# Making the mixture panels on GpSimd alone, with one round of it moved ahead of another panel's low halves

## What is computed

```
xn = layernorm(x)
h = xn @ W.T + b                              # graph part: degree-normalised sum of h over the edges
gnn = segment_sum(norm * h[col], row)
q, k, v = xn @ Wq.T + bq, xn @ Wk.T + bk, xn @ Wv.T + bv
mix = (relu(q P) (relu(k P)^T v)) @ Wo.T + bo   # linear attention, 16 heads of 64
x = x + gnn + mix
x = x + ffn(layernorm(x))                      # 8 experts, gate and up, silu, down, routing weights
```

## Time and profile before

| | |
|---|---|
| median of 3 runs | 1085.24 us (1084.15 to 1086.44) |
| the profiled execution | 1084.87 us, of it the span 1083.1 us |
| TensorE busy | 1062.4 us, 98% |
| VectorE busy | 536.7 us, 50% |
| ScalarE busy | 290.0 us, 27% |
| GpSimd busy | 349.5 us, 32% |
| mean granted clock of TensorE | 0.995 |

### The profile page before, as it was taken

One profiled execution on the slowest core, in us unless ns is written; L12 is line 12 of the kernel. 1 busy time (PEld: TensorE's weight loads), 2 busy tenths in 40 slices (PEclk: granted clock), 3 DMA queues, 4 the chain that ended last, 5 costly groups with the idle time before them and its releaser, 6 DMA issues.

```text
span 1083.1 us, 15216 instructions
## 1 busy us (share of the span) xinstructions
PE 1062.4 (98%) x5527; PEld 882.0 (81%) x5527; DVE 536.7 (50%) x1152; ACT 290.0 (27%) x445; POOL 349.5 (32%) x225
## 2 busy tenths in 40 slices
PE   8999999999999999999959999999999999999998
PEld 7887778887878888888848888887788888888887
DVE  6944666676641222332427657967334212214684
ACT  5320211112232234321222223267222212202221
POOL 4000011122130025375500249955108744500151
PEclk9999999999999999999989999999999999999999
DMA  7303011222233386645595567766045556205912
GB/s 270 98 30 108 13 35 53 62 69 72 70 121 88 141 313 244 234 146 174 169 324 207 204 189 215 197 170 183 1 161 196 206 179 218 64 24 224 378 66 110
DMA packets 135933, 163.17 MB, mean 151 GB/s; under 512 B 8534, under 2 KB 102578, under 8 KB 130738
## 3 DMA queue, kind: packets, MB, share of 16 engines
q1 hardware_dynamic: 135282, 160.33, 44.9%
q10 hardware_dynamic: 576, 1.84, 0.4%
HBM read 107.70 MB, written 54.45 MB: 150 GB/s over the span
## 4 chain that ended last, share of the span: by engine, by line
PE 94%; DVE 3%; DMA 1%; SPq 1%; ACT 1%; issue 1%; ACTq 0%
PE ps L1890 9%; PE ps L1892 9%; PE ps L1891 9%; PE ps L2225 7%; PE ps L2226 7%; PE ps L2227 7%; PE ps L2136 6%; PE ps L2137 6%; PE ps L2138 6%; PE ps L2159 4%; PE ps L2165 4%; PE ps L2056 3%; PE ps L2058 3%; PE ps L2057 3%; PE ps L1900 2%; PE ps L2002 2%
## 5 line engine op out<-in xcount | busy, mean ns | idle before, releaser
L1890 PE MATMUL ps<-w_hi,xnH 128*128 128x512 f32 x464 | 184.6, 398 | 0.0
L1892 PE MATMUL ps<-w_hi,xnL 128*128 128x512 f32 x464 | 180.9, 390 | 0.0
L1891 PE MATMUL ps<-w_lo,xnH 128*128 128x512 f32 x464 | 180.7, 389 | 0.0
L892 POOL TENSOR_TENSOR acc<-acc,cw 128x320 f32<-128x320 f32 x40 | 35.7, 893 | 252.6 <-ACT cw L1096 251.4
L1890 PEld LDWEIGHTS ps<-w_hi,xnH 128*128 128x128 f32 x464 | 87.1, 188 | 18.7
L1892 PEld LDWEIGHTS ps<-w_hi,xnL 128*128 128x128 f32 x464 | 87.1, 188 | 18.6
L1891 PEld LDWEIGHTS ps<-w_lo,xnH 128*128 128x128 f32 x464 | 87.2, 188 | 17.1
L1841 DVE TENSOR_TENSOR prd<-ps,wB 128x512 f32<-128x512 f32 (+1 forms) x24 | 14.2, 593 | 144.5 <-PE ps L2227 105.4
L2056 PE MATMUL ps<-xnH,w_hi 128*128 128x512 f32 (+1 forms) x192 | 68.1, 355 | 0.0
L2225 PE MATMUL ps<-x2H,guH 128*128 128x512 f32 (+1 forms) x192 | 67.7, 352 | 0.4 <-ACT wT L1334 0.4
L2226 PE MATMUL ps<-x2L,guH 128*128 128x512 f32 (+1 forms) x192 | 67.6, 352 | 0.0
(11 more groups left out here) (474 smaller groups left out, 2243.8 us busy)
## 6 DMA issues: line engine op xcount, KB each, us to landing
cR<-c_d SPq DMA_DIRECT2D x20, 640.0 KB, 5.0
foldin<-in SPq DMA_DIRECT2D x32, 256.0 KB, 2.7
guR<-in SPq DMA_DIRECT2D x16, 512.0 KB, 6.8
w_raw<-in SPq DMA_DIRECT2D x14, 512.0 KB, 6.3
c_d<-cw SPq DMA_DIRECT2D x40, 160.0 KB
wdq<-in SPq DMA_DIRECT2D x6, 1024.0 KB, 7.6
qR<-qT_d SPq DMA_DIRECT2D x20, 256.0 KB, 4.9
wd_d<-wd1H SPq DMA_DIRECT2D x5, 1024.0 KB, 6.5
```

The lines of the kernel that those rows point to most:

```text
L1890: pe.matmul(target, xnH[:, kc, cols], wH[w][:, kc, :], start=(kc == 0), stop=False)
L1891: pe.matmul(target, xnH[:, kc, cols], wL[w][:, kc, :], start=False, stop=False)
L1892: mm = pe.matmul(target, xnL[:, kc, cols], wH[w][:, kc, :], start=False, stop=(kc == KC - 1))
```

## The change

- ACT no longer makes the high parts of the mixed panels: `mix_high` and `MIX_AT` are gone. POOL makes them itself with a `tensor_copy` in front of the low part of the same step, and with the two waits that ACT's had (low part of the step before made, high part of the step before stored).
- On POOL, `panel_lo(1)` moves from ahead of the four rounds to between the first and the second round.
- In SyncE's queue, `load_panel(1, wh_pan[1])` and the wait for the last q stores move behind the first four block loads and the first four `own` loads. The wait for M's stores stays ahead of them.

```diff
@@ SyncE
             sp.wait_ge(*made(("q", 23)))
-            load_panel(1, wh_pan[1])
             for p in range(2):
                 sp.wait_ge(m_st[p], 48 * KC)
-            for c in range(3):
-                sp.wait_ge(q_st[c], 16 * KC)
...
             for t in range(4):
                 load_own(t)
+            load_panel(1, wh_pan[1])
+            for c in range(3):
+                sp.wait_ge(q_st[c], 16 * KC)
             for n in range(16):
@@ GpSimd
-            panel_lo(1)
-
             for k in range(4):
...
                     pool.wait_ge(wd_mix, 4 * k + 4)
+                    if n:
+                        pool.wait_ge(wd_lo, n)
+                        pool.wait_ge(wd_st[0], 16 * n)
+                    pool.tensor_copy(mixH[:], mixR[room_of][:]).then_inc(wd_hi, 1)
                     pool.wait_ge(wd_hi, n + 1)
...
+                if k == 0:
+                    panel_lo(1)
@@ ScalarE
-            def mix_high(n):
-                act.wait_ge(wd_mix, 4 * (n // 4) + (1, 3, 3, 4)[n % 4])
-                if n:
-                    act.wait_ge(wd_lo, n)
-                    act.wait_ge(wd_st[0], 16 * n)
-                act.activation(mixH[:], mixR[MIX_MADE[n % 4][0]][:], ACT.Copy).then_inc(wd_hi, 1)
...
-            MIX_AT = {3: (0, 1), 4: (2, 3), 6: (4,), 7: (5, 6), 8: (7,), 9: (8,), 10: (9, 10), 11: (11,), 12: (12,),
-                      13: (13, 14), 14: (15,)}
...
                     h_high(hf, t)
-                    for n in MIX_AT.get(NT * hf + t, ()):
-                        mix_high(n)
```

## The result

| | before | changed |
|---|---|---|
| median of 20 runs | 1085.2 us | 1086.42 us |
| lowest to highest | 1084.15 to 1086.44 | 1084.87 to 1088.05 |
| ratio, 95% interval | | 1.0013 (1.0007 to 1.0018) |
| profiled execution, span | 1083.1 us | 1083.1 us |

The medians are 1.2 us apart and the ratio is 1.0013: within 0.2%, but on the slow side. The forecast was 1086.1 us.

A forecast was written before the change was run, and what follows sets the result against it. The bound was the end of the 16 steps (537.56), then 21.7 us to the first of the seven products. Terms -2.8 + 1.0 + 0 + 1.9, plus 0.8 for overlaps, gave +0.9 us: 1086.1 us, range 1081.3 to 1091.5.

The forecast's parts named there:

- round 2: From round 1's last combination to round 2's: 13.8 us to the last low store against 13.83 before, so 0.
- overlaps, put apart: Added 0.8 us for loads stretched beside DVE's work and more POOL operations on the chain in each round.
- The bound: End of the 16 steps sets the time, us for us, through TensorE's 11.1 us wait; at most about 10 us winnable.
- The rival by which the q loads are bound by tile 9's h: A tie for another reason: no move of the chain of steps would show in the time; no chance given.
- The copy: POOL's cast of 128 by 512, 16 times on the chain, put at 0.63 us each.
- The dearer copy: Rival: POOL's copy at 0.95 us adds 5.1 us, giving 1091.2; copy or overlaps dearer had chance 0.22.
- the rival that would have made the time 1088.3: POOL's copy takes the skill's 769 ns, making the sum 2.2 us longer; chance 0.10.
- Round 0 and the low halves: POOL starts at 449.2, 11.7 us earlier; panel 1's 10.83 us of low halves leave 2.8 us at round 1's checkpoint.
- The rival of a kept lead: Panel 1's low halves do not hold round 1's start, -8.8 us remains, time 1076; chance 0.03 with other surprises.
- The links: Copy to copy on POOL: copy 0.63, hop 0.1, store 2.65, so 3.4 us; 3.2 in round 3.
- the rival of faster stores: High and low parts' stores land in 2.4 us, links take 3.15, time 1082.3 to 1083.1; chance 0.18.
- The covers: Three edits cost nothing: ACT without mix_high, panel load 5.3 us later with 2 us left, low halves 15 us early.

The follow-up runs named there:

- e1: The changed kernel again, unaltered, for a second trace and more times: 1086.17 us against 1085.75 for the kernel before, ratio 1.0009.
- e7: Changed kernel with each of the 16 copies made twice: 1095.37 us against 1085.4 for the kernel before, ratio 1.0094.
- e2: Kernel before with only the copies moved to GpSimd, old order of SyncE and low halves: 1089.18 us against 1085.75, ratio 1.0034.
- e3: Changed kernel with the copies back on ACT: 1083.84 us against 1085.75 for the kernel before, ratio 0.9983.
- e4: Changed kernel with two of panel 1's four low halves moved to between rounds 1 and 2: 1084.58 us, ratio 0.9996 to the kernel before.
- e9: Changed kernel with each of the first products waiting only for its own q tile: 1086.28 us against 1085.56 before, ratio 1.0009.
- e10: Changed kernel with per-tile q waits, split low halves and 15 filling products in TensorE's wait: 1084.55 us against 1085.56 before, ratio 0.9996.
- e8: Changed kernel with 45 unused products in TensorE's wait before the seven products: 1084.33 us against 1085.4 before, ratio 0.9998.
- the four: Traces of the changed kernel, e1, e8 and e9, which have the same 16 steps; their last low stores average 538.4.
- e12: e11 with the last q tile loaded ahead of the second panel in SyncE's queue: 1077.45 us against 1085.33 for the kernel before, ratio 0.9927.
- e11: e10 with the copies on ScalarE (ACT): 1081.38 us against 1085.56 for the kernel before, ratio 0.9960.
- e5: Changed kernel with the first mixed panel and q tiles 0 to 8 loaded early from ACT's queue: 1085.54 us against 1085.4 before, ratio 1.0002.

## Why the prediction was right

The median lies 0.3 us from the forecast. Two terms were off by 0.6 to 0.8 us or more and in opposite directions, so part of that closeness is luck; the terms can be read one by one. Last combinations of rounds 1, 2, 3 and last low store, as differences to before:

| term | forecast | first trace | e1's trace |
|---|---|---|---|
| start to round 1 | -2.8 | -3.5 | -3.3 |
| round 1 | +1.0 | +0.9 | +0.8 |
| round 2 | 0 | +0.8 | +2.0 |
| round 3 and last store | +1.9 | +1.5 | +1.8 |
| overlaps, put apart | +0.8 | (in the rounds) | (in the rounds) |
| sum | +0.9 | -0.2 | +1.3 |

- *The bound.* One wait, one slope: e7 (+9.1 us at the last store, about +9 us of time) and e2 (+4.0, +3.4) show it upwards. Downwards the sign holds and less comes out: e3 (-3.3, -1.9), e4 (-3.1, -1.2); the table of traces shows the clock's part in it. The rival by which the q loads are bound by tile 9's h falls with e2 and e7. What the forecast did not see is that a second limit, the last q tile, stands directly behind the first one. It did no harm, since both move with the last low store; it would have spoiled every forecast of an edit in the last stretch, as it did mine for e9 and e10.
- *The copy.* Put at 0.63 us; it is 0.61 (16 rows, 0.61 to 0.62). The line to 512 elements went through two different operations, so that it lay within 0.02 us is in part luck. The dearer copy (0.95 us) falls. With the cast of 64 elements (0.236 us) this one gives 0.83 ns an element and 0.18 us fixed. The Trainium skill ("GPSIMD Engine Reference", section 3.1) puts a body of at most two operations at 1.03 cycles an element, 0.86 ns at the 1.2 GHz that it counts with, and the traces agree. Its 769 ns for 512 elements in the best unrolled loop, the rival that would have made the time 1088.3, is not what this cast takes.
- *Round 0 and the low halves.* The start came 0.6 us earlier than put (448.6 for 449.2), the end of round 0 and the 10.4 us of low halves as put (467.8 and 478.2 for 468.0 and 478.8). e4 shows that this is a place where the lead of 12 us goes: half of the low halves moved away gave 5.7 us back at the next last combination. The rival of a kept lead fell with the 10.4 us.
- *The links.* Put at 3.4 us (3.2 in round 3). In the trace, in rounds 1 to 3: 3.24, 3.68, 3.47; 3.15, 3.14, 4.15; 3.12, 3.11, 3.11. The prediction called itself wrong if the links of rounds 1 and 2 are not 3.4 to 3.9: their means are (3.46 and 3.48), four of the six single ones are not, so the spread of the links was not foreseen. The landings in a quiet queue are the rival of faster stores (2.3 us, median of the stores from 500 us on), and it happens in part of the links (3.1 us is a copy with a quiet landing); in rounds 1 and 2 others were slower. Round 2, where I put 0, cost 0.8 and 2.0 us: my zero leaned on round 2 of the kernel before, in which a high store took 4.2 us to land, and in the changed kernel's round 2 a low store took 4.4 us (issued at 510.19, the load behind it at 514.57), in e1's 5.4 us (510.30, 515.67). That is the one term that was clearly mis-sized, and the 0.8 us for overlaps covered it, in the main for a reason that I had not given. Operations were stretched too: in the first trace some two-input ones (1.29 to 1.62 us) and no cast, but in e1's trace of the same kernel a cast beside DVE's work took 0.90 us, and in e8 and e9 two and three of the 16 took 1.0 to 1.1:

```profile
533.47 0.90 POOL L934 CAST mixH<-mix0R 128x512 fp32r<-128x512 f32 x1 [1.12 <-DMA mt_d<-mixH]
```
```profile
533.14 0.75 DVE L1628 SCALAR_TENSOR_TENSOR xnL<-htmp,dis,xnH 128x512 fp32r<-128x512 f32 x1 [0.79 <-ACT xnH L1176]
```

- *The covers.* All three held. ACT's first high part of panel 1 came at 454.14 (put: 454) and the banks were free in time; TensorE has no wait in the h stage.
- *The clock* was left as it was, rightly for the change, but its size was read from one row: 1.6 us there. In six traces (before, changed, e1 to e4) the products after the wait ran at the lower level, 1.2 GHz, for 3.1 to 6.1 us, without relation to the length of the wait, so 1.5 to 3 us were lost, and e8 puts the whole at about 2 us.
- *The two parts* were forecast as one sum. Alone they are +3.4 us (e2) and -1.9 us (e3), together +0.4 to +1.2: they add up within the intervals.

Open: why single landings in a round take 4 us and more in place of 2.3 to 2.9 was not tried. The kernel before has one trace, so how far its own last low store moves between executions is not known, and the 0.8 us between it and the mean of the four is no better than that. The difference of the two medians of the changed kernel against before (+1.2 in 20 runs, +0.4 in e1) is within the intervals.

## What to carry to other kernels

Cut a chain of small round trips at the engine that would have been idle: the same copy at the same price (0.61 to 0.63 us, 16 times) cost 3.4 us when it moved from an engine that made it beside the chain to one that makes it in line. Work started 12 us earlier is worth only what is not given back at the next fixed block in the same queue, so follow the lead checkpoint by checkpoint to the last one. And before a wait is shortened, look for the second limit behind it: here it was fed by the same queue, a finer wait alone won nothing (e9), and the change of the queue's order won 3.9 us (e12 against e11).

## What the runs showed of the hardware that I had not expected

- 6.5 MB of loads beside the chain made 16.7 us of delay in it (e5): the median landing of a 256 KB store went from 2.3 to 3.5 us. Behind the chain, the part of them that TensorE waited for took 18.7 us. Moving them under it was worth nothing.
- A 256 KB store issued behind 2 MB of loads in the same queue took 7.9 us (e3), three times the 2.3 of a quiet queue.
- The granted clock came back from 1.2 to 2.4 GHz 3.1 to 6.1 us after the first product behind a wait, in no order with the wait's length: 3.1 after 11.9 (e1), 6.1 after 7.4 (e3), 5.2 after 14.5 (e2).
- DVE's two-input operation of 128 by 512 (L1628) takes 0.75 us alone and up to 2.87 us beside GpSimd's subtraction of the low halves (at 467.92 in the changed kernel). GpSimd's one-input cast of the same width was slowed less often: in none of 16 in the first trace, in one of 16 in e1 (0.90 us), in two of 16 in e8 and three of 16 in e9 (1.0 to 1.1 us, for 0.61).
